# Spreading and gating the slot-table scatters on GpSimd in a fused attention and mixture-of-experts kernel

## The reference

```python
h = h + attention(layernorm(h))      # 16 query heads, 4 key/value heads of 32
h = h + ffn(layernorm(h))            # 64 experts, top 6, 64 places each, and a shared expert

# inside ffn, for every token:
scores = softmax(x @ gate_w.T); topk_w, topk_i = top_k(scores, 6)
pos   = rank of this (token, expert) pair among all pairs of its expert
valid = pos < 64
buf[expert, pos] = x[token]          # where valid
y = (silu(buf @ w_gate) * (buf @ w_up)) @ w_down
out = sum over the six of y[expert, pos] * topk_w * valid  +  shared(x)
```

## Time and profile before

| | |
|---|---|
| median of 3 runs | 1630.76 us (1613.08, 1630.76, 1630.90) |
| profiled execution, its own time | 1628.74 us |
| its span, first to last instruction | 1626.9 us |
| mean granted TensorE clock | 0.866 |
| PE busy | 1323.2 us, 81% |
| DVE busy | 748.0 us, 46% |
| ACT busy | 397.1 us, 24% |
| POOL busy | 426.1 us, 26% |

### The profile page before, as it was taken

How to read it: one execution, slowest core, us unless ns; L and a number is a source line. 1 busy time by engine, 2 the same in 40 slices (tenths; PEclk the granted TensorE clock), 3 DMA queues, 4 the chain that set the end, 5 groups by cost and what they waited for, 6 DMA issues and landing times. The chain is left out here.

```text
span 1626.9 us, 23852 instructions
## 1 busy us (share of the span) xinstructions
PE 1323.2 (81%) x9072; PEld 829.1 (51%) x9072; DVE 748.0 (46%) x1658; ACT 397.1 (24%) x660; POOL 426.1 (26%) x455
## 2 busy tenths in 40 slices
PE   3095788988888888898887501999999999999994
PEld 2095453535345453535343401667666666766662
DVE  7983657464765756565653213222222233222330
ACT  3111223324343432424343102111121111111110
POOL 3000100201115243341524763122222222222221
PEclk8598777878799988979799655999999999999997
DMA  3023221314241413323232405989797989889782
GB/s 102 0 56 83 56 57 37 76 37 115 53 102 42 115 38 100 75 59 96 59 96 70 176 25 146 334 274 296 255 337 242 311 266 321 274 286 291 255 246 33
DMA packets 131630, 239.54 MB, mean 147 GB/s; under 512 B 59977, under 2 KB 65881, under 8 KB 131545
## 3 DMA queue, kind: packets, MB, share of 16 engines
q1 hardware_dynamic: 116024, 214.16, 42.1%
q0 software_dynamic: 15520, 24.22, 7.5%
HBM read 175.66 MB, written 38.90 MB: 132 GB/s over the span
## 5 line engine op out<-in xcount | busy, mean ns | idle before, releaser
L947 DVE TENSOR_REDUCE at_maxes<-at_ps 128x1 f32<-128x384 f32 x384 | 196.4, 552 | 105.6 <-PE at_ps L665 102.7
L805 ACT ACTIVATE bulk<-at_ps 128x1152 f32<-128x1152 f32 x128 | 144.6, 1129 | 361.9 <-PE at_ps L637 360.6
L1329 PE MATMUL mo_ps<-mo_x2s,mo_sgu 128*117 128x384 f32 (+1 forms) x1152 | 220.6, 344 | 0.0
L1329 PEld LDWEIGHTS mo_ps<-mo_x2s,mo_sgu 128*117 128x117 f32 (+1 forms) x1152 | 198.3, 181 | 13.2 <-issue 13.1
L1550 POOL DMA_INDIRECT out_rows<-mo_y,mo_scatter_ix x64 | 91.3, 1427 | 398.2 <-DMA out_rows<-mo_y,mo_scatter_ix 227.0
L1130 POOL DMA_INDIRECT slot_table<-at_toki,at_si x144 | 141.3, 981 | 50.4 <-issue 46.5
L665 PE MATMUL at_ps<-at_qb 32*128 32x384 bf16 x384 | 107.6, 395 | 32.6 <-DVE at_maxes L947 19.3
L628 PE MATMUL at_ps<-WxT,at_xT 128*128 128x512 f32 (+1 forms) x576 | 113.4, 349 | 11.4 <-ACT at_v L847 9.6
L1093 POOL TENSOR_TENSOR at_oTs<-at_oT,at_oTs 128x384 fp32r<-128x384 f32 x32 | 31.9, 1010 | 310.3 <-ACT at_oTs L821 310.3
L665 PEld LDWEIGHTS at_ps<-at_qb 32*128 32x128 bf16 x384 | 26.9, 94 | 163.0 <-DVE at_maxes L947 130.1
L628 PEld LDWEIGHTS at_ps<-WxT,at_xT 128*128 128x128 f32 x576 | 89.6, 192 | 39.1 <-issue 25.0
(11 more groups left out here) (198 smaller groups left out, 1658.1 us busy)
## 6 DMA issues: line engine op xcount, KB each, us to landing
mo_wgu<-in_L_ffn_w_gate SPq DMA_DIRECT2D x32, 704.0 KB
mo_wgu<-in_L_ffn_w_up SPq DMA_DIRECT2D x32, 704.0 KB
bulk<-in_L_ffn_w_gate SPq DMA_DIRECT2D x32, 704.0 KB, 7.1
bulk<-in_L_ffn_w_up SPq DMA_DIRECT2D x32, 704.0 KB, 8.5
mo_wd<-in_L_ffn_w_down SPq DMA_DIRECT2D x32, 512.0 KB
bulk<-in_L_ffn_w_down SPq DMA_DIRECT2D x32, 512.0 KB, 5.4
at_QT<-at_qhi SPq DMA_DIRECT2D x64, 192.0 KB
rows_scores<-at_x SPq DMA_DIRECT2D x8, 864.0 KB, 3.9
```

Of the source, the lines that this page charges most:

```text
L805: A.activation(PT[:, N % RING, :, :], ps[:, 0:NT, 0:SEQ], ACT.Exp, scale=float(HD) ** -0.5)\
L947: V.tensor_reduce(maxes[:, half, s, h:h + 1], ps[:, 5 + u % 2, 0:SEQ], AX.X, ALU.max, negate=True)\
L1329: m = M.matmul(ps[0:SW[c], 5 + g, 0:SEQ], sgu[:, wa, g, k, SO[c]:SO[c] + SW[c]], x2s[:, xa, k, :], start=(k3 == 0), stop=(k3 == 3 * KC - 1))
```

## The change

Before, slots 7 to 12 held three scatters each. After, slots 7 to 15 hold two each, again 18. In iterations with `main`, each pair also waits for `probs_ready` to reach 16 b + n, that is for the exponential of slot n - 1 to be done. In iterations 8 to 10 there is no such wait, and only the distribution over the slots is another: nine scatters stood ahead of `places(d)`, which has its place at the head of slot 10, and nine behind; after the change six stand ahead of it and twelve behind. Slot 15's pair stands behind that slot's two `out_lo`, and ahead of all that slot 0 of the next iteration holds.

```diff
-                    if prev3 and 7 <= n <= 12:
+                    if prev3 and n >= 7:
                         pool.wait_ge(slots_ready, e + 1)
-                        for m in range(3 * (n - 7), 3 * (n - 6)):
+                        if main:
+                            pool.wait_ge(probs_ready, NH * b + n)
+                        for m in range(2 * (n - 7), 2 * (n - 6)):
                             G.indirect_dma_start(slot_table, bass.IndirectOffsetOnAxis(ap=si[:, m:m + 1], axis=0),
                                                  toki[:, m // TOPK:m // TOPK + 1], None, bounds_check=NSLOT - 1,
                                                  oob_is_err=False, compute_op=ALU.bypass).then_inc(scattered, 16)
```

## The result

| | before | after |
|---|---|---|
| median of 20 runs each | 1626.07 us (1613.08 to 1633.43) | 1633.70 us (1623.91 to 1644.80) |
| ratio after to before | | 1.0047 (95% interval 1.0026 to 1.0067) |
| profiled execution, its span | 1628.74, 1626.9 us | 1631.56, 1629.6 us |
| granted clock, PE busy | 0.866, 1323.2 us | 0.866, 1317.8 us |

The change makes the kernel 7.6 us slower; 8.5 were forecast. The forecast of 1639 us was made on the three runs shown then, whose median was 4.7 us over that of the twenty. On a chip of another kind the same change turned out faster by 0.8%; that is told with the last runs.

What follows compares the result with a forecast made beforehand. Bound: one chain over POOL from iteration 7 to the slot table read, steady part unchanged. Tail delays 2.5 + 2.15 + 3.8 = 8.45, say 8.5 us, on 1630.76 gave 1639 us; 8 in 10 for 1620 to 1650.

Steps and rivals of the forecast that it cites:

- Bound and place: Steady iterations 3 to 6 change by nothing; the POOL chain from iteration 7 to the slot table read gets longer.
- Term 1: Turn from iteration 7 to 8: slot 15's pair delays the inverse deviation on POOL, +2.5 us.
- Term 2: Iteration 8: twelve scatters behind `places` instead of nine, `places` 1.67 us earlier; next inverse deviation +2.15 us.
- Term 3: Iteration 9: three scatters leave POOL's 5.11 us idle time and stand behind `places`, +3.8 us.
- The sum: Tail, iterations 7 to 9: the three delays add to 8.45 us, say +8.5, 0.5% slower.
- Holds cost nothing: Steady iterations: waits for the exponential cost 0; `places` late by a microsecond isn't felt, its output being used an iteration later.
- Rival A: Steady part: pacing the bursts gains at most 8.5 us, cancelling the tail's loss, 1630 us; chance 0.07.
- Rival D: Tail from iteration 8's `places`: POOL's instruction refill pause falls into the open, adding 2.3 or 4.6 us; chance 0.14.
- Rival B: Every iteration: slot 15's pair delays slot 0's `out_lo` and inverse deviation, 10.2 us on top, 1649 us; chance 0.04.
- Rival C: Tail: another wait covers the delays of iterations 7 and 8, only iteration 9's 3.8 us stands, 1635 us; chance 0.07.
- Rival E: Steady iterations: the granted clock moves the sum by up to 12.5 us either way, 1626 or 1651; chance 0.10.
- Rival F: Steady part: holds already met when POOL reaches them; tail and time as forecast; included in the forecast's 0.58.

Runs made afterwards that it cites:

- e2: Changed kernel with its holds and pairs in iterations 3 to 6 alone, iterations 7 to 10 as before; ratio to the kernel before 1.0004.
- e10: Kernel before with all 18 scatters of iteration 9 behind `places`; table read 126.33 us after iteration 7's last exponential, 111.59 in the kernel before.
- e1: Changed kernel without its waits for the exponential, spread over slots 7 to 15 kept; ratio to the kernel before 1.0063.
- e3: Kernel before with the waits for the exponential alone, three scatters in slots 7 to 12 kept; ratio 0.9995.
- e8: Kernel before with thirteen scatters ahead of `places` in iteration 9, two buffers for slot and token numbers, a semaphore each; median 1618.21 us, ratio 0.9961.
- e9: Kernel before with ten scatters in slots 7 to 10 and eight in slot 15, iterations 3 to 6, without holds; ratio 1.0092.
- e7: Kernel before with thirteen scatters ahead of `places` in iteration 9 and five behind, in place of nine and nine; ratio 0.9979.

## Why the prediction was right, and where it wasn't

- **Bound and place.** Right: on chips A the steady part is worth nothing that shows either way (e2: 1.0004), and the table read ends the only chain that the change lengthens.
- **Term 1, the pair of slot 15 of iteration 7**: +2.23 for +2.5. The step said that the pair's 2.55 us pass on less 0.08. The third `out_lo` started 2.48 us later, as the pair took 2.28 (879.40 to 881.68) and began 0.2 us later than that `out_lo` had; and the inverse deviation, which had 0.18 us of idle time ahead of it, now follows with none.
- **Term 2, iteration 8**: +2.24 for +2.15, the tie between POOL and DVE and the 1.67 us that `places` gains included.
- **Term 3, iteration 9**: +3.88 for +3.8, and the same price per scatter in the other direction (-4.64 for four, 5.1 less 0.4 by which `places` started later, the thirteenth scatter not quite fitting) and, with the pause counted, for nine (e10: +13.5 for 11.5 + 2.3).
- **The sum**: +8.31 to the table read for +8.5, and 7.6 us in the median. The spans differ by 2.7 only, 1629.6 - 1626.9: the profiled execution after reached iteration 7's last exponential 4.5 us sooner, mostly by its clock (0.91 against 0.85 in iteration 1, which took 79.41 and 84.03 us), and 1.1 us went between the read and the end. In the twelve other traces "rest" lies between 634.3 and 636.1, so 1.1 us is of the size of the spread, though the 634.07 here is its lower end.
- **Holds cost nothing, a late `places` in a steady iteration isn't felt**: e1 and e3, on chips A.
- **Rival A, a gain in the steady part**, was weighed by one trace from one kind of chip, and there it is rightly 0. "Scatters cost a steady iteration nothing that shows" holds on chips A alone. On chips B a scattering iteration of the kernel before takes 94.9 us against 92.0 for iteration 2, and the gain ahead of the tail is 23.7 us, some 6 of them the clock's, where I had put 8.5 as its most. The step that failed is the bound: it was drawn from the spread of iterations that never showed the pauses.
- **Rival D**: the pause is there and costs 2.3 us in the open (e10), but not for the reason that was quoted. The Trainium skill, "Runtime: NRT & Kernel Launch", section "Instruction fetch mechanics", says that instructions are refilled in blocks of 256. If the pause were such a refill, added instructions would have moved it. It stands ahead of the 57th and the 113th of the 144 scatters in the kernel before and in the changed one, which has 45 instructions more, all on POOL (29 of them ahead of the 57th scatter), and in all other traces but that of e8. In the changed kernel the 113th still lies ahead of `places` of iteration 9, so no pause came into the open, as the forecast had it. It goes by the number of scatters, not by instructions.
- **Rival B**: its price, 10 us, is excluded on chips A by e2, which has the pair of slot 15 in iterations 3 to 6. Its condition, what a delay larger than POOL's idle time costs, stays without a clean test, since e9 ran where another effect covers it.
- **Rival C** fell with the three runs of one iteration each. **Rival E**: single traces do reach iteration 7's last exponential 4.5 us apart and more; over 20 runs of each kernel this stays inside the interval of the ratio. **Rival F**: the holds are not met when POOL comes to them (51.3 us of waiting), and by e1 this changes nothing in the tail.

## What to carry to other kernels

Work on an engine that is off the critical path in the steady loop may be on it in the pipeline's last iterations: what is spread evenly over slots there moves from a hidden idle time to behind the instruction that everybody waits for. Decide the order of the last iterations by itself, and fill the idle time ahead of a wait (e8, -6.8 us to the read). Count a change from the latest event that both traces share, since the granted clock moves single traces by as much as the effect; and before a kernel is tuned on a burst of small indirect DMAs, look at it on more than one chip: the same change was 0.47% slower on one kind and 0.78% faster on the one chip of another kind where it ran.

## What the runs showed of the hardware that wasn't expected

- On chips B (two chips, kernel before 1652 to 1653 us against 1625 to 1626) ACT and DVE, and PE with them, pause while POOL runs through a series of indirect DMAs, in the case read above with a finished producer; the trace names "remote" or "issue" as the releaser, and most of these waits are of 3 to 7 us. No trace from chips A has a "remote" release at all; that of the kernel before on a chip B has 13, spread over all five iterations from 3 to 7, that of the changed kernel one. In the four traces of chips B, 34 such waits are longer than 1 us, and each overlaps scatters: in a series of nine ahead of `places` the fifth to the ninth, never the first four alone. What stands still (a semaphore's arrival, the fetch of instructions, the records themselves) isn't settled, nor why only some chips show it. Nor is it known which half of the change removes the pauses, the holds or the spread over more slots: each was run alone on chips A only. The version with two buffers wasn't run on a chip B; it has the bursts of the kernel before in iterations 3 to 8 and so may keep the pauses there, and the changed kernel's steady part with e8's tail is the version that the two sets of runs point to, and was not run.
- POOL pauses 2.26 to 2.31 us ahead of its 57th and 113th indirect DMA of the phase, wherever these stand, in 13 of 14 traces. The exception is e8, where neither pause is there (0.30 us at both); it has two semaphores in place of one, each of which gets half the increments, and two buffers, and the same thirteen scatters ahead of `places` as e7, which has both pauses. Which of these does it wasn't tried, nor what POOL waits for.
- One scatter of 128 words costs POOL 1.27 us from start to start, and DVE sees the last one 1.2 us after its end, alike on all chips; the durations of the scatters are the same on both kinds (median 971 to 973 ns).
